# Whole-row value groups in the small attention: one group of values per key tile behind two rounds of scores and maxima

## The chip, the core and the metric

The kernel runs on one core of one Trainium2 chip. The metric is device time of one execution in microseconds (us), from the first to the last instruction of the core. The engines are TensorE (PE; its weight loads are PEld), VectorE (DVE), ScalarE (ACT), GpSimd (POOL) and SyncE (SP), which issues most DMAs. TensorE's clock is granted at 1.2 or 2.4 GHz; "granted clock 1.00" is 2.4.

## The reference, cut to what matters

Four sequences of S = 512 tokens, D = 256 features, pass through six blocks: a transformer block with rotary attention and 16 experts, a small attention, the first block again, a recurrent "thought" block, a windowed attention, and the thought block again. The change lies in the small attention:

```python
x = x + _L0_attn_ref(_layernorm(x, axis=-1), ...)
# in it: 32 query heads, 8 key/value heads, head size 8, no mask
q = q.reshape(B, S, 32, 8).transpose(0, 2, 1, 3)
k = jnp.repeat(k, 4, axis=1); v = jnp.repeat(v, 4, axis=1)
scores = jnp.einsum('bhqd,bhkd->bhqk', q, k) * scale
attn = jax.nn.softmax(scores, axis=-1)
out = jnp.einsum('bhqk,bhkd->bhqd', attn, v)
return out @ Wo + bo
```

## The kernel before

A plan (`Plan`) is written first: a list of steps in one order. Each engine's program then walks the same list and issues what it has to do for each step, so the order of the list is the order on every engine, and each engine waits in order. PSUM has eight banks of 128 partitions by 512 fp32 values.

The small attention (`small_attention`) works on batch b (4), query-head group qt (4), key/value head kv = 2 qt + g (8), key tile kt (T = 4 tiles of 128 keys), and r (KV = 4), the four query heads that share kv. Heads are eight wide (SD = 8), and the parts of the split fp32 operands are stacked to 24 rows, so that four matmuls for r = 0 to 3 fit into the four groups of 32 rows of TensorE's array and run side by side.

- `attend` (matmul at L1630): scores of one key tile (128 partitions) against all 512 queries, 26 rows, with the stored maxima among them, into a bank of `tring` (three banks, 3 to 5). ScalarE takes the exponential into a slot of `prT` (12 slots, L1844) and frees the bank.
- `maximum` (L1618): scores of a query tile against all keys, 24 rows, into a bank of `sring` (three banks, 0 to 2). VectorE reduces each to its maximum (L2034) and frees the bank. Maxima run ahead of the attends by a lead of 48. After 32 of them VectorE splits them into parts (L2040 to L2043), and four rounds' steps later TensorE turns them (`store_maxima`, L1624) through the single bank of `wring` (bank 7); ScalarE (L1840) and a DMA of POOL store them. In batch 0, four extra maxima follow each qt.
- `value` (L1641): the values, 32 columns wide for each r, so that four matmuls stand side by side in the four column groups, 128 rows deep, against the exponentials. They add up over four key tiles in the one bank of `oring` (bank 6), and in fp32 each is two records of the trace. In front of them, for kt > 0, stand matmuls of bf16 zeros (L1639), which add nothing to the sum. After the last key tile ScalarE copies the bank to `o_sb` (L1848).
- `finish` (L1649): four transposes of `o_sb` through `wring`, then VectorE divides by the row sums (L2049, L2051).
- Side work, one step of a generator `beside()` after every second attend: the products and values of the next batch (`small_product` L1599 to L1603, whose last, L1603, is followed by ScalarE's and VectorE's parts L1836 and L2022 out of `wring`; `small_values` L1609 to L1611; `feature` L1521), and the output products of the last batch (`small_out`, L1656 to L1658). All of it uses `wring`.

The inner loop yields after each attend; one maximum follows it, and after r = 1 and r = 3 a side step. Then `tick()` counts down the list `later` and runs what is due. The two halves of the values of key tile kt are due at the third and fourth tick after the last attend of kt. So the order on TensorE is: half 0, two scores and two maxima, side step, half 1, two scores and two maxima, side step. The halves are queries 0 to 255 and 256 to 511. Each half of kt > 0 has eight zero matmuls of 256 columns, two rounds over the four column groups.

Of the kernel before, what the change touches and what calls it, by code (L numbers as in the profile page):

```python
# [8 lines left out]
B, S, D = 4, 512, 256  # L9
T = S // P  # L10
# [4 lines left out]
KV = 4  # L15
# [13 lines left out]
VR = 32  # L29
# [123 lines left out]
def cols(c0, n):  # L153
    return slice(c0, c0 + n)


class Plan:
# [791 lines left out]
    def small_attention(self, ph, ahead):  # L949
# [5 lines left out]
        A = Phase()  # L955
# [14 lines left out]
        s = self.step("small_constants", A)  # L970
        s.after, s.count = self.boundary, self.count(f"p{ph}_const")
        const = s.count.up(64)
        s = self.step("small_fill", A)
# [15 lines left out]
        s = self.step("small_bias", A)  # L989
# [29 lines left out]
        s = self.step("small_ones", A)  # L1019
# [6 lines left out]
        stack_ready, stack_read, v_aug_of, v_ready, o_tm_of, o_made, nm_done = {}, {}, {}, {}, {}, {}, {}  # L1026
# [117 lines left out]
        later = []  # L1144
# [8 lines left out]
        def attend(b, qt):  # L1153
            if qt == 0:
                o_tm_of[b], o_made[b] = o_tm.take(), None
            otm, va = o_tm_of[b], v_aug_of[b]

            def value(kv, kt, exps, ob, half):
                if not ob:
                    ob.append(oring.take())  # L1160
                s = self.step("value", A)
                s.kv, s.kt, s.exps, s.use, s.va, s.v_ready, s.half = kv, kt, exps, ob[0], va.ap, [v_ready[b]], half
                s.o = None
                if half == 0:
                    return
                weighed = s.use.full if kt == T - 1 else self.values_weighed.up()
                for pt, _ in exps:
                    pt.users.append(weighed)
                if kt == T - 1:
                    s.o = o_sb.take()  # L1170
                    if kv % 2 and qt == 3:
                        stack_read[b] = s.use.full
                        va.users.append(s.use.full)
                    later.append([2, lambda: finish(kv, s.o, s.use.free)])

            def finish(kv, o, copied):
                s = self.step("finish", A)
                s.kv, s.o, s.copied, s.use, s.rr, s.otm = kv, o, copied, wring.take(), rsum.take(), otm
                o.users.append(s.use.full)
                s.inverted = self.vector_made.up()  # L1180
                s.rr.users.append(s.use.free)
                o_made[b] = s.use.free

            for g in range(2):
                kv = qt * 2 + g
                ob = []
                for kt in range(T):
                    exps = []
                    for r in range(KV):
                        s = self.step("attend", A)  # L1190
                        s.b, s.kv, s.kt, s.r, s.ready = b, kv, kt, r, [nm_done[b, qt], ones_there]
                        s.use, s.pt = tring.take(), prT.take()
                        exps.append((s.pt, s.use.free))
                        pace[0] = s.use.free
                        if r == KV - 1:
                            for half in range(2):
                                later.append([2 + half, lambda kv=kv, kt=kt, exps=exps, ob=ob, half=half: value(kv, kt, exps, ob, half)])
                        yield
                        if r % 2:
                            tick()  # L1200
# [306 lines left out]
def tensor_program(pe, plan):  # L1507
# [4 lines left out]
    for s in plan.order:  # L1512
        A = s.of
# [3 lines left out]
        elif s.kind == "feature":  # L1517
            w.wait_ge(s.use.before)
            for t in range(T):
                w.wait_ge(s.ready[t])  # L1520
                ins = pe.transpose(s.use.ap[:, t * P:(t + 1) * P], s.srcs[t], ident[:, :])  # L1521
            ins.then_inc(s.use.full[0].sem)

        elif s.kind in ("q_product", "q_rotate"):
# [5 lines left out]
            for k in range(KC):  # L1530
# [3 lines left out]
                ins = pe.matmul(use.ap[:, 0:n], hi, wlo[:, k, cols(c0, n)], start=False, stop=k == KC - 1)  # L1534
            ins.then_inc(use.full[0].sem)

        elif s.kind == "q_turn":
            w.wait_ge(s.use.before, s.ready)
            for j in range(QW // P):
                ins = pe.transpose(s.use.ap[:, j * P:(j + 1) * P], s.tm.ap[:, j * P:(j + 1) * P], ident[:, :])  # L1540
            ins.then_inc(s.use.full[0].sem)

        elif s.kind == "k_turn":
            w.wait_ge(s.use.before)
            for g in range(A.nk):
                ins = pe.transpose(s.use.ap[:, g * P:(g + 1) * P], s.tm.ap[:, QW + g * P:QW + (g + 1) * P], ident[:, :])
            ins.then_inc(s.use.full[0].sem)

        elif s.kind == "scores":
# [5 lines left out]
            for i, (qp, kp) in enumerate(((0, 0), (4, 0), (0, 1))):  # L1555
                for h in s.heads:
                    rows = slice(0, P) if A.wide else cols(h.j % 2 * A.hd, A.hd)
                    at = qp + (h.j if A.wide else (o.g * KV + h.j) // 2)
                    ins = pe.matmul(h.use.ap[:, 0:n], q[rows, at, :], k[rows, kp, o.g, keys], start=i == 0, stop=i == 2)  # L1559
# [3 lines left out]
        elif s.kind == "turn":  # L1563
            o = s.o
            w.wait_ge(s.use.before)
            for j in range(KV):
                w.wait_ge(o.norms[j])
                ins = pe.transpose(s.use.ap[:, j * P:(j + 1) * P], o.probs[j].ap[:, s.kt * P:(s.kt + 1) * P], ident[:, :])  # L1568
# [63 lines left out]

        elif s.kind == "value":
            w.wait_ge(s.use.before, A.zeroed, *s.v_ready)
            part = cols(s.half * S // 2, S // 2)
            for j, (pt, made) in enumerate(s.exps):
                if j == 0 and s.kt:
                    for i in range(2 * KV):
                        pe.matmul(s.use.ap[cols(i % KV * VR, VR), part], A.zero[:, 0:VR], A.zero[:, part], start=False, stop=False)  # L1639
                w.wait_ge(made)  # L1640
                ins = pe.matmul(s.use.ap[VR * j:VR * (j + 1), part], s.va[:, s.kt, s.kv, :], pt.ap[:, part],  # L1641
                                start=s.kt == 0 and s.half == 0, stop=s.kt == T - 1 and s.half == 1)
            if s.half:
                ins.then_inc(s.use.full[0].sem if s.kt == T - 1 else plan.values_weighed.sem)

        elif s.kind == "finish":
            w.wait_ge(s.use.before, s.copied)
# [995 lines left out]
```

## Time and profile before

| | us |
|---|---|
| median of 3 runs | 3684.36 (3679.31 to 3690.25) |
| the profiled execution, its span | 3687.3 |
| PE busy | 3303.7 (90%) |
| DVE busy | 2631.0 (71%) |
| ACT busy | 1933.5 (52%) |
| POOL busy | 990.3 (27%) |
| TensorE's mean granted clock | 0.938 |

The profiled execution was not timed apart from its span. Busy times are unions over the span; a matmul's time holds its latency, so a busy TensorE is not one at its peak. "Idle before" is an engine's idle time just ahead of an instruction, with the instruction of another engine that ended it; "issue" is a wait for nothing that the profile shows. In the timeline each line is a group of like instructions: start, time from the first start to the last end, engine, line of the kernel, operation, output and input, and the count.

### The profile page before, as it was taken

How to read it: one execution, taken by the hardware profiler on the slowest of the kernel's cores; microseconds unless marked ns; L12 is line 12 of the kernel's file. 1: busy time of each engine (PE TensorE's matmuls, PEld its weight loads, DVE VectorE, ACT ScalarE, POOL GpSimd, SP SyncE). 2: the span in 40 equal slices, each digit the busy share in tenths (PEclk: the TensorE clock that was granted, in tenths of full speed). 3: DMA queues.
4: the chain of work that ended last, by engine and by line, in shares of the span. 5: the costliest groups of instructions: out<-in, count | busy, mean ns of one | idle time of the engine just before them, and what ended most of it. 6: DMA issues, size and time to landing. Idle time of an engine off the chain costs nothing. (4 is left out here: it accounts for less than half of the span.)

```text
span 3687.3 us, 65201 instructions
## 1 busy us (share of the span) xinstructions
PE 3303.7 (90%) x22154; PEld 2194.8 (60%) x22154; DVE 2631.0 (71%) x8703; ACT 1933.5 (52%) x5275; POOL 990.3 (27%) x960
## 2 busy tenths in 40 slices
PE   6999999987997899997899999988799749999975
PEld 4666767664554344445667667665455437887853
DVE  5888888885444788873788888887344567777755
ACT  4667767664222366774676767666222125555531
POOL 3211112233454001012121212143444332222213
PEclk8999999998998689997999999998899769999986
DMA  4140500013755322302060500011756300000010
GB/s 129 52 170 7 166 1 1 20 48 110 178 91 116 70 46 58 73 23 72 1 220 1 172 1 1 4 48 57 215 88 122 89 1 15 1 16 4 1 34 23
DMA packets 202239, 234.78 MB, mean 64 GB/s; under 512 B 20662, under 2 KB 188536, under 8 KB 201080
## 3 DMA queue, kind: packets, MB, share of 16 engines
q1 hardware_dynamic: 170968, 190.48, 17.0%
q0 software_dynamic: 30944, 40.14, 6.5%
q8 instruction: 181, 2.97, 0.3%
q14 instruction: 146, 1.20, 0.1%
HBM read 98.13 MB, written 133.73 MB: 63 GB/s over the span
## 5 line engine op out<-in xcount | busy, mean ns | idle before, releaser
L1816 ACT ACTIVATE p_prob<-bank,p_small 128x256 f32<-128x256 f32 (+3 forms) x1280 | 646.2, 515 | 156.0 <-DVE p_small L1988 151.3
L1988 DVE CUSTOM_DVE_ANT_0 bank<-bank,p_mask 128x256 f32<-128x256 f32 (+3 forms) x1280 | 579.0, 490 | 97.1 <-PE bank L1559 85.7
L2336 POOL TENSOR_TENSOR p_tm<-p_rope_a,p_rope_b 128x512 f32<-128x512 f32 x192 | 245.8, 1280 | 1269.0 <-DVE p_rope_b L1968 1264.5
L1559 PE MATMUL bank<-p_k,p_q 64*128 64x256 f32 (+3 forms) x3840 | 529.2, 347 | 13.6 <-ACT p_prob L1816 12.5
L1821 ACT ACTIVATE p_prT<-bank 128x512 f32<-128x512 f32 x752 | 426.0, 601 | 211.5 <-PE bank L1568 209.6
L1568 PE MATMUL bank<-g_ident,p_prob 128*128 128x128 f32 x3008 | 438.3, 284 | 54.4 <-DVE p_prob L1997 20.8
L1997 DVE TENSOR_SCALAR p_prob<-p_prob,p_small 128x256 f32<-128x256 f32 (+3 forms) x1280 | 424.5, 395 | 11.3
L1577 PE MATMUL bank<-p_prT,p_v 128*64 128x512 f32 (+1 forms) x1504 | 428.2, 619 | 0.3 <-ACT p_prT L1821 0.3
L1568 PEld LDWEIGHTS bank<-g_ident,p_prob 128*128 128x128 f32 x3008 | 330.0, 142 | 150.6 <-issue 50.2
L1559 PEld LDWEIGHTS bank<-p_k,p_q 64*128 64x128 f32 (+1 forms) x3840 | 339.1, 188 | 116.1 <-issue 65.1
L2034 DVE TENSOR_REDUCE p_nmax<-bank 128x1 f32<-128x512 f32 x512 | 320.8, 683 | 56.8 <-PE bank L1618 54.6
L1844 ACT ACTIVATE p_prT<-bank 128x512 f32<-128x512 f32 x512 | 278.1, 597 | 132.1 <-PE bank L1630 129.7
L1751 PE MATMUL bank<-p_w,p_hT 128*128 (+1 forms) x632 | 325.7, 598 | 0.1
L1532 PE MATMUL bank<-p_w_hi,p_aT_hi 128*128 128x512 f32 (+1 forms) x768 | 287.5, 374 | 5.5 <-DVE p_aT_lo L1930 4.6
L1816 ACT ACTIVATION_READ_ACCUMULATOR p_prob<-bank,p_small 128x1 f32 x1280 | 267.3, 209 | 0.0
L1533 PE MATMUL bank<-p_w_hi,p_aT_lo 128*128 128x512 f32 (+1 forms) x768 | 266.4, 347 | 0.0
L1534 PE MATMUL bank<-p_w_lo,p_aT_hi 128*128 128x512 f32 (+1 forms) x768 | 265.9, 346 | 0.0
L1825 ACT ACTIVATE p_oT_hi<-bank 128x512 fp32r<-128x512 f32 x192 | 114.8, 598 | 242.1 <-PE bank L1577 240.3
L1589 PE MATMUL bank<-p_o_hi,p_oT_hi 128*128 128x256 f32 x768 | 226.4, 295 | 5.8 <-DVE p_oT_lo L2002 5.8
L1965 DVE TENSOR_TENSOR p_rope_a<-bank,p_cos 128x512 f32<-128x512 f32 (+1 forms) x384 | 186.7, 486 | 62.4 <-PE bank L1534 60.8
L1577 PEld LDWEIGHTS bank<-p_prT,p_v 128*64 128x64 f32 (+1 forms) x1504 | 126.7, 148 | 169.4 <-issue 161.1
L1590 PE MATMUL bank<-p_o_hi,p_oT_lo 128*128 128x256 f32 x768 | 216.7, 282 | 0.0
(288 smaller groups left out, 6215.8 us busy)
## 6 DMA issues: line engine op xcount, KB each, us to landing
sorted<-p_blank SPq DMA_DIRECT2D x32, 2304.0 KB, 19.2
p_w<-in_L_ffn_w SPq DMA_DIRECT2D x96, 256.0 KB, 4.5
p_h_in<-sorted SPq DMA_DIRECT2D x158, 144.0 KB, 2.7
p_k_st<-k_saved SPq DMA_DIRECT2D x16, 288.0 KB
p_q_st<-q_saved SPq DMA_DIRECT2D x16, 288.0 KB
g_stage<-in_L_ffn_wq SPq DMA_DIRECT2D x8, 512.0 KB, 3.8
g_stage<-in_L_ffn_wo SPq DMA_DIRECT2D x16, 256.0 KB, 4.3
q_saved<-p_qp SPq DMA_DIRECT2D x16, 256.0 KB, 3.2
```

Of the source, the lines that this page charges most:

```text
L1532: pe.matmul(use.ap[:, 0:n], hi, whi[:, k, cols(c0, n)], start=k == 0, stop=False)
L1533: pe.matmul(use.ap[:, 0:n], lo, whi[:, k, cols(c0, n)], start=False, stop=False)
L1559: ins = pe.matmul(h.use.ap[:, 0:n], q[rows, at, :], k[rows, kp, o.g, keys], start=i == 0, stop=i == 2)
L1568: ins = pe.transpose(s.use.ap[:, j * P:(j + 1) * P], o.probs[j].ap[:, s.kt * P:(s.kt + 1) * P], ident[:, :])
L1577: ins = pe.matmul(s.use.ap[cols(o.g * A.hd, A.hd), :], o.u.v.ap[:, o.k0 + kt, cols(o.g * A.hd, A.hd)], o.prT[kt].ap, start=kt == 0, stop=k ...
L1751: ins = pe.matmul(o.up.ap, o.hT.ap[:, k * P:(k + 1) * P], w_all(A)[:, bass.ds(at + k * 2 * H, 2 * H)], start=k == 0, stop=k == KC - 1)
L1816: act.activation(s.prob.ap[:, 0:s.o.w], s.use.ap[:, 0:s.o.w], ACT.Exp, bias=sm[:, 0, j:j + 1], scale=-1.0, accum_out=sm[:, 1, j:j + 1]).th ...
L1821: act.activation(s.prT.ap, s.use.ap, ACT.Copy).then_inc(s.use.free[0].sem)
L1844: act.activation(s.pt.ap, s.use.ap, ACT.Exp).then_inc(s.use.free[0].sem)
L1988: dve.tensor_tensor_reduce(x, x, A.mask[:, A.mask.shape[1] - o.w:], -1.0, FAR, ALU.add, ALU.min, o.sm.ap[:, 0, h.j:h.j + 1]).then_inc(made)
L1997: dve.tensor_scalar(o.probs[j].ap[:, 0:o.w], o.probs[j].ap[:, 0:o.w], o.sm.ap[:, 2, j:j + 1], None, ALU.mult).then_inc(made)
L2034: dve.tensor_reduce(A.nmax[:, s.qt % 2, s.t, s.r, s.g % 2:s.g % 2 + 1], s.use.ap, axis=AX.X, op=ALU.max, negate=True).then_inc(s.use.free[ ...
```

## The change

The two halves of `value` become one step, due at the third tick. It issues one round of four zero matmuls of 512 columns for kt > 0 (in place of four rounds of four with 256 columns), then four value matmuls over all 512 queries. Nothing else is touched: the rings, the number of rounds, the lead and the side steps stay. `finish` is still put into `later` by the step of the last key tile, which now runs one tick earlier.

```diff
-            def value(kv, kt, exps, ob, half):
+            def value(kv, kt, exps, ob):
                 if not ob:
                     ob.append(oring.take())
                 s = self.step("value", A)
-                s.kv, s.kt, s.exps, s.use, s.va, s.v_ready, s.half = kv, kt, exps, ob[0], va.ap, [v_ready[b]], half
+                s.kv, s.kt, s.exps, s.use, s.va, s.v_ready = kv, kt, exps, ob[0], va.ap, [v_ready[b]]
                 s.o = None
-                if half == 0:
-                    return
...
                         if r == KV - 1:
-                            for half in range(2):
-                                later.append([2 + half, lambda kv=kv, kt=kt, exps=exps, ob=ob, half=half: value(kv, kt, exps, ob, half)])
+                            later.append([2, lambda kv=kv, kt=kt, exps=exps, ob=ob: value(kv, kt, exps, ob)])
...
         elif s.kind == "value":
             w.wait_ge(s.use.before, A.zeroed, *s.v_ready)
-            part = cols(s.half * S // 2, S // 2)
+            if s.kt:
+                for i in range(KV):
+                    pe.matmul(s.use.ap[cols(i * VR, VR), :], A.zero[:, 0:VR], A.zero[:, :], start=False, stop=False)
             for j, (pt, made) in enumerate(s.exps):
-                if j == 0 and s.kt:
-                    for i in range(2 * KV):
-                        pe.matmul(s.use.ap[cols(i % KV * VR, VR), part], A.zero[:, 0:VR], A.zero[:, part], start=False, stop=False)
                 w.wait_ge(made)
-                ins = pe.matmul(s.use.ap[VR * j:VR * (j + 1), part], s.va[:, s.kt, s.kv, :], pt.ap[:, part],
-                                start=s.kt == 0 and s.half == 0, stop=s.kt == T - 1 and s.half == 1)
-            if s.half:
-                ins.then_inc(s.use.full[0].sem if s.kt == T - 1 else plan.values_weighed.sem)
+                ins = pe.matmul(s.use.ap[VR * j:VR * (j + 1), :], s.va[:, s.kt, s.kv, :], pt.ap,
+                                start=s.kt == 0, stop=s.kt == T - 1)
+            ins.then_inc(s.use.full[0].sem if s.kt == T - 1 else plan.values_weighed.sem)
```

## Rows read from the trace of the kernel before

**Rows 1.** Windows: length, busy us (instructions) by engine, PEclk, DMA share, GB/s.

```profile
1249.70:1694.70 445.00, 419.99 (x4984) 200.65 (x4983) 333.79 (x636) 306.91 (x577) 51.06 (x78) 0.94 0.20 47
1522.95:1533.84 10.89, 10.47 (x149) 4.96 (x148) 10.23 (x18) 8.69 (x17) 0.00 (x0) 1.00 0.77 191
```

**Rows 2.** Timeline of one clean pair; start, us, engine, line, operation, count.

```profile
1522.95 0.40 PE L1639 MATMUL bank<-p_zero 128*32 128x256 bf16 x8
1523.18 0.60 PE L1641 MATMUL bank<-p_prT,p_v_aug 128*32 128x256 f32 x8
1523.72 0.50 PE L1618 MATMUL bank<-p_k_st,p_q_st 24*128 24x512 f32 x1
1524.15 0.40 PE L1639 MATMUL bank<-p_zero 128*32 128x256 bf16 x8
1524.27 1.90 DVE L2034 TENSOR_REDUCE p_nmax<-bank 128x1 f32<-128x512 f32 x3 [0.28 <-PE bank L1618]
...
1525.45 0.40 PE L1639 MATMUL bank<-p_zero 128*32 128x256 bf16 x8
```

**Rows 3.** Groups by line, 1260 to 1690: count, busy us, mean ns, idle before.

```profile
L2034 DVE TENSOR_REDUCE p_nmax<-bank 128x1 f32<-128x512 f32 x448 | 281.6, 683 | 52.5 <-PE bank L1618 50.3
```

**Rows 4.** Timeline where extra maxima follow one another.

```profile
1306.43 6.87 DVE L2034 TENSOR_REDUCE p_nmax<-bank 128x1 f32<-128x512 f32 x11
...
1309.65 0.18 PEld L1618 LDWEIGHTS bank<-p_k_st,p_q_st 24*128 24x128 f32 x1 [0.50 <-DVE p_nmax L2034]
```

**Rows 5.** Waits (us, times, longest), then TensorE's timeline with side work.

```profile
PEld bank L1641 <- ACT p_o_sb L1848: 14.2, 22, 0.8
...
1547.16 0.30 PE L1609 MATMUL bank<-p_w_hi,p_uT_hi 128*128 128x64 f32 x1
...
1547.95 0.40 PE L1639 MATMUL bank<-p_zero 128*32 128x256 bf16 x8
...
1567.07 0.50 PE L1630 MATMUL bank<-p_q_st,p_k_st 26*128 26x512 f32 x1
...
1568.03 0.49 PE L1618 MATMUL bank<-p_k_st,p_q_st 24*128 24x512 f32 x1
...
1569.73 0.39 PE L1656 MATMUL bank<-p_w_hi,p_oT_hi 128*128 128x256 f32 x1
...
1570.63 0.64 PE L1641 MATMUL bank<-p_prT,p_v_aug 128*32 128x256 f32 x8
```

**Rows 6.** Timeline of a bias product with `finish` behind it.

```profile
1503.47 0.39 PE L1603 MATMUL bank<-p_ones,p_b_st 2*64 2x512 f32 x1
...
1504.64 0.59 ACT L1836 ACTIVATE p_qp<-bank 64x512 fp32r<-64x512 f32 x1
...
1505.26 0.68 DVE L2022 SCALAR_TENSOR_TENSOR p_qp<-bank,p_qp 64x512 fp32r<-64x512 f32 x1 [0.27 <-ACT p_qp L1836]
...
1505.99 0.66 PE L1649 MATMUL bank<-g_ident,p_o_sb 128*128 128x128 f32 x4 [1.05 <-DVE p_qp L2022]
```

**Rows 7.** Windows around changes of the granted clock.

```profile
1200.00:1250.00 50.00, 37.28 (x99) 18.51 (x101) 44.64 (x106) 7.20 (x11) 5.66 (x7) 0.53 0.45 101
...
1307.60:1311.30 3.70, 3.29 (x29) 1.36 (x32) 3.70 (x7) 2.05 (x4) 0.00 (x0) 1.00 0.80 171
...
1312.50:1316.80 4.30, 4.00 (x46) 1.49 (x43) 2.91 (x6) 2.84 (x6) 0.00 (x0) 0.60 0.10 23
...
1341.50:1352.00 10.50, 10.47 (x133) 4.84 (x132) 9.49 (x20) 7.60 (x15) 2.22 (x4) 1.00 0.02 5
...
1366.66:1381.70 15.04, 13.62 (x97) 5.57 (x96) 10.10 (x21) 7.41 (x14) 2.22 (x4) 0.51 0.02 3
...
1645.00:1656.80 11.80, 11.32 (x151) 5.16 (x150) 3.08 (x15) 9.76 (x20) 5.33 (x8) 1.00 0.02 4
```

**Rows 8.** Timeline at half clock.

```profile
1251.49 1.08 PE L1641 MATMUL bank<-p_prT,p_v_aug 128*32 128x256 f32 x8
...
1252.51 0.79 PE L1618 MATMUL bank<-p_k_st,p_q_st 24*128 24x512 f32 x1
```

## Prediction

> **What bounds the kernel now.** I read the windows first, then the groups by line, then the timeline of the one stage that the change touches, tile by tile. The values are computed only in the small attention, between 1249.7 and 1694.7 us of the 3687.3 us span: 445 us, with TensorE busy 420, VectorE 334, ScalarE 307, mean granted clock 0.94 [rows 1]. Whatever the change does must come out of these 445 us; the other 3242 us keep their instructions and their order.
>
> TensorE looks like the bound (94% busy), but its busy time counts latency. A stretch without side work shows what sets the pace: the eight half-groups of kv 1522.95 to 1533.84 take 10.89 us, with VectorE busy 10.23 us of them [rows 1]. There is one `value` half per round of scores and maxima, and the pair of halves of one key tile takes 1522.95 to 1525.45, 2.50 us [rows 2]. Four reduces at 0.63 us of engine time each (281.6 us / 448) are 2.51 us [rows 3]. So in clean stretches the maxima on VectorE set the pace already; TensorE alone would need 2 x 1.20 = 2.40 us (zeros 0.23, values 0.54, scores 0.43 from start to start [rows 2]). Only where side work (products, transposes, output products) stands between the rounds is TensorE itself the bound.
>
> **The change part by part.** Call A the round with r = 0, 1 and B that with r = 2, 3, each two scores and two maxima. Before: values half 0, A, side slot 1, values half 1, B, side slot 2. After: whole values, A, side slot 1, B, side slot 2. There are 128 key tiles, hence 128 such pairs (1024 fp32 value matmuls of 256 queries, two records each; 1536 zero matmuls).
>
> *Zeros.* 96 key tiles have them. Before, a half has 8 matmuls x 256 columns, four column groups side by side, and costs 0.23 us: 0.46 us a tile. After, 4 x 512 columns in one round: the same columns per group as one half, so 0.23 us. TensorE is spared 0.23 us a tile. Off TensorE nothing changes.
>
> *Values.* A half costs 0.54 us to the next scores, of which 4 x 256 columns at 2.4 GHz (two records deep, two passes each) are 0.43 and 0.11 is the turn to the scores. A whole is 0.85 + 0.11 = 0.96, behind zeros 1.19 us. Bounds: 1.07 us (no turn, no start-up) and 1.37 us (two halves as now), 0.12 us below and 0.18 us above; I take 1.19 because half-clock rows (1.08 us for eight records against 0.60) scale with the columns and not with the instructions [rows 2, 8].
>
> *Scores.* One turn scores-to-values (0.43 - 0.21 = 0.22 us) and one back (0.11) disappear per tile. With the zeros that is 0.56 us a tile for TensorE alone, 2.40 to about 1.85 us. If TensorE were the only bound this would be some 65 us.
>
> *Where the gain goes.* The maxima have three PSUM banks (`sring`), the scores three (`tring`). Two adjoining rounds need four of each. The second maximum of B takes the bank of the first maximum of A, and TensorE is in order, so it waits for that reduce. From the rows: scores start 1523.72, reduce starts 1524.27, 0.55 us later [rows 2]; one reduce lasts 0.68; the weight load follows 0.06 us behind the freed bank. The last is seen where extra maxima stand in a row: the eleven reduces from 1306.43 are 0.62 us apart, the fifth ends at 1309.59, and the next load starts at 1309.65, waiting for VectorE [rows 4]. So B's last maximum starts 0.55 + 0.68 + 0.06 = 1.29, say 1.30 us behind A. Behind it the values queue (0.43 later), and behind the values (1.19) the next A. A clean pair becomes 1.30 + 0.43 + 1.19 = 2.92 us, whatever TensorE saved. VectorE has its four reduces from 0.55 to 3.11 us (0.68 + 3 x 0.62) and the next fill at 2.92 + 0.55 = 3.47: it now idles 0.36 us per pair. The bound has become a loop from bank to bank. On ScalarE the same loop is 0.53 + 0.60 + 0.06 = 1.19 us, just under it; it governs the last pairs, where the maxima have ended. The Trainium skill, TensorEngine Tiling, "PSUM Bottleneck" and the first of its gotchas, says that tiled matmuls move the bottleneck to the copies out of PSUM and that row tiling presses on the banks. By that rule alone nothing is gained in clean stretches; by the same page's "Key Properties", that a change of tiling mode drains the engine, the turns saved would count. The trace agrees with both (0.22 and 0.11 us of turn, and the waits for L2034).
>
> *Pair by pair*, from the timeline (S-to-S starts; d1, d2 are the side work in the slots). After = values + max(1.30, 0.43 + d1) + 0.43 + d2.
> - 17 clean pairs at 2.50: 2.92, +7.1. Five more behind the last maxima, 2.43 to 2.81: +1.9.
> - 7 pairs with VectorE's three small maxima parts, 2.88 to 3.0: +0.8.
> - 13 pairs with the last key tile, 2.99: the second 0.5 us there is the next values' wait for the single output bank (14.2 us over 22 waits [rows 5]). It goes, since two rounds now hide the 0.6 us copy, but the pair is 2.92 (2.81): -1.1.
> - 17 pairs with the first key tile (no zeros, 1.00 us) and the `finish` transposes, 2.89. One tick earlier, `finish` now falls into slot 1, inside the bank wait, and is free: 1.00 + 1.30 + 0.43 = 2.73: -2.7.
> - 9 pairs with products in both slots (0.79 to 0.84 each [rows 5]), about 4.06 to 3.73: slot 1 lies inside the wait, slot 2 in full: -3.0.
> - 9 pairs with output products in slot 2 alone (0.90 [rows 5]), 3.41 to 3.82, 4.33 to 4.78: +3.5.
> - 10 pairs with the store of maxima (L1624 splits A by 0.96 [rows 5]), 7 up 0.15, 3 with products down 0.35: 0.
> - 6 pairs where the bias product (L1603) is followed by `finish`, 4.02 us. `finish` needs the one `wring` bank, which ScalarE and VectorE must empty first: L1603 at 1503.47, ScalarE's part at 1504.64, VectorE's ends 1505.94, transposes 1505.99, a wait of 1.05 us behind B [rows 6]. Now `finish` is asked for in slot 1, ahead of B, and holds B up: 1.61 (A's two exponentials) + 0.55 + 0.68 puts it 2.85 us behind A, then 0.59 + 0.43 + 1.06, with 1.00 of values: 4.9 us. +5.4. Behind `finish` are queued B's four matmuls, and VectorE starves with them.
> - The rest (transposes in slot 1, -1.2; output products with `finish`, -0.9; three pairs with four extra maxima of batch 0, +1.5; bias product alone, +0.6; eight half-clock pairs, +2.4): +2.4.
>
> Sum: +14.3 us at the clock of before.
>
> *The clock.* It falls to 1.2 GHz behind stretches with little TensorE work: 1307.60 to 1311.30 (3.7 us with one half of values) is followed by 0.60 in 1312.50 to 1316.80, and 1362.99 to 1366.66, a stretch like it, by 0.51 over 15 us [rows 7]. There are four such stretches in the timeline, where batch 0 has its extra maxima; three were followed by a fall, one (1337.86) was not: 1.00 in 1341.50 to 1352.00 [rows 7]. A fall costs 1.3 to 5.6 us (the half-clock pairs against like pairs), 3.2 on the mean. The six `finish` pairs now have 3.9 us without values each; I count three more falls, +10 us.
>
> The profiled execution spans 3687.3 us, within the runs' 3679.3 to 3690.3 and 0.08% over their median, so I add to the median: 3684.4 + 14.3 + 10 = 3709 us, some 0.7% slower.
>
> **The rivals.**
> 1. *The gain arrives* (faster). If the second maximum of B did not wait (rounds spread by side work, or reduces that run ahead), clean pairs stay at VectorE's 2.50, last-tile and first-tile pairs fall to 2.50 (30 x 0.45 = 14 us), and the 35 pairs with side work fall by 0.5 (17 us): -31 us, 3653 us. For it: VectorE is only 75% busy in the stage. Against: three banks and four maxima are in the code, and the wait is in rows 4. It decides if B's last maximum starts under 0.9 us behind A, where the clean pair is 2.50.
> 2. *It cancels* (no change). The value group at its low bound (-0.12 x 128 = -15 us) and no more falls: 3684 us.
> 3. *The clock gives way.* Values and zeros are the matmuls over all 128 rows; they stream 0.85 + 0.43 of a clean pair's 2.50 us now (0.51), 0.85 + 0.21 of 2.92 then (0.36), since half the zeros are gone and the pair is longer; with scores alone the clock stood at 0.53 over 1200 to 1250 while TensorE was 75% busy [rows 7]. At half clock zeros and values are 0.43 + 1.71 + 0.15 = 2.29, the bank loop 0.86 (0.55 and the scores' 0.79 us against 0.50 [rows 2, 8]) + 0.68 + 0.06 = 1.60, scores 0.73: 4.62 us a pair, +1.70. With 40% of the pairs there: +87 us, about 3785 us. Against: the clock held 1.00 in 1645.00 to 1656.80, with two matmuls a round [rows 7]. The Trainium skill, TensorE: Matmul & The Clock Gate, "A second HAM failure mode: psum-queue depth-cycling", says that small idles between groups that cycle through PSUM banks make the clock swing; this change makes just such idles. By that rule the time would be this rival's.
> 4. *It doesn't do what it says*: then L1639 would not show x384 and L1641 not x1024. The diff leaves no room for that, and it gets no chance.
>
> **How the numbers follow.** Forecast (+12 to +45 us) 0.50; rival 1 0.16; rival 2 0.20; rival 3 0.14. The predicted time is the first's, 3709. The values' upper bound (0.18 x 128 = 23 us) and eight falls in all (25 us) make 3746; on top the range goes on into rival 3, to 3768. Below, it takes in rival 2 and a third of rival 1's gain, 3674. A difference of 0.3% (11 us) is about what a measurement of this kernel can tell from no change. Faster 0.17, same 0.20, slower 0.63.
>
> **What would show it.** L1639 x384 at 512 columns, L1641 x1024. Right: the last L1618 of B starting 1.3 us behind A with its load waiting for L2034; clean pairs of 2.9 us; VectorE idle about 0.36 us a pair before L2034; L1848 no longer ahead of L1641; L1649 waiting some 2 us for L2022 six times. Wrong: clean pairs of 2.5 us, or a mean clock in the stage under 0.85.

## The result and the profile after

The changed kernel takes 3733.99 us (median of 4 runs, 3728.65 to 3737.49), the kernel before 3686.8 us on the same chip (4 runs): a ratio of 1.0132, 95% interval 1.0114 to 1.0151, slower by 47 us. The forecast was 3709 us, slower by 25 us (by 22 us once the kernel before has its fourth run). The direction and the range held; the size was half of what came. The slowdown is 1.3%, clear of no change by its interval but small.

The page of the changed kernel (busy us and share of the span; then by line: busy us, mean ns, idle before):

```profile
span 3726.9 us, 60853 instructions
PE 3316.3 (89%) x19976; PEld 2160.4 (58%) x19978; DVE 2628.5 (71%) x8703; ACT 1931.7 (52%) x5275; POOL 991.6 (27%) x960
...
L2029 DVE TENSOR_REDUCE p_nmax<-bank 128x1 f32<-128x512 f32 x512 | 320.5, 683 | 86.7 <-PE bank L1615 85.8
```

TensorE has 2178 instructions fewer and is busy 12.6 us longer. VectorE's reduces (L2034 before, L2029 now) cost the same, but VectorE idles 86.7 us ahead of them; before it was 56.8.

The stage, from the first to the last value matmul, and parts of it (length, busy us by engine, granted clock):

```profile
1256.20:1743.50 487.30, 432.42 (x2808) 166.85 (x2807) 332.85 (x636) 302.44 (x577) 51.13 (x78) 0.87 0.19 43
1256.20:1360.00 103.80, 91.68 (x570) 34.75 (x569) 76.72 (x143) 59.24 (x112) 6.68 (x12) 0.86 0.23 51
1360.00:1450.00 90.00, 79.87 (x447) 27.87 (x445) 60.95 (x110) 48.62 (x93) 6.68 (x12) 0.72 0.18 40
1450.00:1545.00 95.00, 85.24 (x640) 36.75 (x639) 79.64 (x154) 65.74 (x127) 9.83 (x17) 1.00 0.12 26
1545.00:1700.00 155.00, 137.26 (x983) 56.51 (x981) 113.90 (x225) 104.05 (x204) 22.14 (x36) 0.96 0.22 52
1700.00:1743.50 43.50, 38.37 (x184) 10.97 (x176) 1.65 (x6) 24.79 (x45) 5.81 (x2) 0.57 0.11 31
```

It is 487.3 us long where it was 445.0 [rows 1], 42 us more; the profiled span grew by 39.6 us (the stage starts 6 us later, and the rest behind it is 9 us shorter; neither holds changed code). The clock is 0.87 in place of 0.94. Since the clock has two levels, (1 - clock) x 2 x length is the time at 1.2 GHz: 127 us of the stage now, 53 us before (the clock's two digits leave some 5 us open; its own records in the traces add up to 130 and 49 us).

**A clean pair at full clock.** In the timeline of the changed kernel (start, us, what it is, count, idle before) L1634 are the zeros, L1637 the values, L1627 the scores, L1615 the maxima:

```profile
1505.78 0.40 PE L1634 MATMUL bank<-p_zero 128*32 128x512 bf16 x4
1506.01 1.03 PE L1637 MATMUL bank<-p_prT,p_v_aug 128*32 128x512 f32 x8
...
1508.71 0.40 PE L1634 MATMUL bank<-p_zero 128*32 128x512 bf16 x4
1508.94 1.03 PE L1637 MATMUL bank<-p_prT,p_v_aug 128*32 128x512 f32 x8
...
1509.90 0.49 PE L1615 MATMUL bank<-p_k_st,p_q_st 24*128 24x512 f32 x1
...
1510.49 2.06 ACT L1839 ACTIVATE p_prT<-bank 128x512 f32<-128x512 f32 x4 [0.86 <-PE bank L1627]
1511.14 0.50 PE L1627 MATMUL bank<-p_q_st,p_k_st 26*128 26x512 f32 x1 [0.52 <-ACT p_prT L1839]
1511.21 0.50 PE L1615 MATMUL bank<-p_k_st,p_q_st 24*128 24x512 f32 x1
1511.64 0.40 PE L1634 MATMUL bank<-p_zero 128*32 128x512 bf16 x4
```

The pair is 2.93 us (1505.78 to 1508.71 and again to 1511.64); the forecast was 2.92. Zeros cost 0.23, values 0.96. The wait in the second of the two pairs: round A starts at 1509.90; the last maximum of round B starts 1.31 us later, and the zeros and values behind it 0.43 us after that. Ahead of it stands a score that waits for ScalarE: the exponential's bank comes free at 1.24 us, the maximum's at 1.3.

**Half clock.** A like pair, 139 us earlier:

```profile
1366.53 0.62 PE L1634 MATMUL bank<-p_zero 128*32 128x512 bf16 x4
1366.92 1.93 PE L1637 MATMUL bank<-p_prT,p_v_aug 128*32 128x512 f32 x8
1368.78 0.79 PE L1627 MATMUL bank<-p_q_st,p_k_st 26*128 26x512 f32 x1
...
1370.32 0.79 PE L1627 MATMUL bank<-p_q_st,p_k_st 26*128 26x512 f32 x1 [0.32 <-ACT p_prT L1839]
1370.39 0.79 PE L1615 MATMUL bank<-p_k_st,p_q_st 24*128 24x512 f32 x1
1371.10 0.62 PE L1634 MATMUL bank<-p_zero 128*32 128x512 bf16 x4
```

It is 4.57 us (forecast 4.62), 1.64 us more. Of 127 pairs 28 are at half clock; in the kernel before it was 11 (counting only pairs that are at half clock for more than half of their length, 26 and 10).

**The `finish` behind the bias product** (L1644 the transposes, L2017 VectorE's part of the product):

```profile
1531.31 0.39 PE L1600 MATMUL bank<-p_ones,p_b_st 2*64 2x512 f32 x1
...
1532.47 0.58 ACT L1831 ACTIVATE p_qp<-bank 64x512 fp32r<-64x512 f32 x1
1533.09 0.68 DVE L2017 SCALAR_TENSOR_TENSOR p_qp<-bank,p_qp 64x512 fp32r<-64x512 f32 x1 [0.26 <-ACT p_qp L1831]
...
1533.83 0.66 PE L1644 MATMUL bank<-g_ident,p_o_sb 128*128 128x128 f32 x4 [2.13 <-DVE p_qp L2017]
```

TensorE stands for 2.13 us where it stood for 1.05 [rows 6]; the pair, 1529.97 to 1534.85, is 4.88 us (forecast 4.9). Another of the six, with the same wait, is 5.65 us long because the clock falls in the middle of it, at 1434.0:

```profile
1434.71 1.12 PE L1644 MATMUL bank<-g_ident,p_o_sb 128*128 128x128 f32 x4 [2.15 <-DVE p_qp L2017]
```

The four transposes take 1.12 us there and not 0.66.

### The profile page after: what moved, and what is told of

It reads as the page before. It is cut to its first block and busy times, and to the rows that moved or that the text cites. A ratio compares the mean times of both kernels' runs of the same rounds, so it can differ in the third digit from the quotient of the medians.

```text
span 3726.9 us, 60853 instructions
## 1 busy us (share of the span) xinstructions
PE 3316.3 (89%) x19976; PEld 2160.4 (58%) x19978; DVE 2628.5 (71%) x8703; ACT 1931.7 (52%) x5275; POOL 991.6 (27%) x960
## 5 line engine op out<-in xcount | busy, mean ns | idle before, releaser
L2029 DVE TENSOR_REDUCE p_nmax<-bank 128x1 f32<-128x512 f32 x512 | 320.5, 683 | 86.7 <-PE bank L1615 85.8
```

The lines of the kernel that those rows point to most:

```text
L2029: dve.tensor_reduce(A.nmax[:, s.qt % 2, s.t, s.r, s.g % 2:s.g % 2 + 1], s.use.ap, axis=AX.X, op=ALU.max, negate=True).then_inc(s.use.free[ ...
```

## The experiments

The ratio of each run is to the kernel before on the same chip. Three chips were used: the first for e1 to e4, the second for e5 to e8, the third for e9 to e11. On the last two the kernel before itself took 3723 us and not 3684 (the same instructions), so of whole times only ratios are compared. The stage can be compared across chips: the changed kernel's is 487.3 us in the first profile and 483.5 on the third chip (e11), while the rest of the execution is 3240 and 3270 us. A time that was expected is set against 3684 us times the ratio. "At half clock" is worked out from the stage's window as above. Two theories of the clock stood against each other, beside the bank loop that both share: that the clock follows the zero columns (theory 1), or the idle time behind the bank wait (theory 2).

**e1, e7, e10: the kernel before with other numbers of zeros.**

```diff
-                    for i in range(2 * KV):
+                    for i in range(KV):       # e1; e7: range(3 * KV); e10: the whole "if j == 0 and s.kt" left out
```

> The kernel before (values in two halves), with one round of four zero matmuls of 256 columns ahead of each half in place of two. Both theories: clean pairs stay at 2.50 us, since VectorE's four reduces set them; a pair with products in both slots goes from 4.1 to 3.9 us. Theory 1, the bank loop costs at full clock and the missing zeros cost the clock: half-clock pairs, 12 in the kernel before, rise towards the 28 of the changed kernel, and the time is 3700 to 3720 us. Theory 2, the idle time behind the bank wait and not the zeros costs the clock: half-clock pairs stay near 12, and the time is 3675 to 3685 us, the saved zeros where side work binds (about 40 pairs by 0.2 us).

> The kernel before with three rounds of zeros of 256 columns ahead of each half in place of two (e1 had one). Theory 1, that the clock follows the zero columns: e1 21, before 11, so about 5 half-clock pairs here, 8 us less, against 0.21 us more for each of 96 pairs that TensorE bounds (up to 20 us): 3685 to 3697 us. Theory 2: half-clock pairs unchanged from 11, 3697 to 3705 us.

> The kernel before without any zeros. Theory 1: the clock follows the zero columns (three rounds 11 half-clock pairs, two 11, one 21), so 35 or more half-clock pairs here and 1.003 to 1.010 of the kernel before, though TensorE is spared 0.46 us in each of 96 pairs. Theory 2: half-clock pairs near 11 to 15, and a ratio under 0.997, since side pairs fall by 0.46 us and clean pairs to VectorE's 2.39.

Ratios: none 1.0096 (1.0061 to 1.0131), one round 1.0018 (1.0001 to 1.0035), three 1.0026 (1.0010 to 1.0041). The stage of e10, no zeros (window: length, busy us by engine, granted clock):

```profile
1276.70:1740.60 463.90, 441.18 (x3448) 184.40 (x3447) 332.85 (x636) 306.01 (x577) 51.08 (x78) 0.81 0.20 45
```

The stage of e1, one round:

```profile
1257.40:1708.40 451.00, 426.09 (x4216) 193.93 (x4215) 333.07 (x636) 306.68 (x577) 51.08 (x78) 0.89 0.20 46
```

The stage of e7, three rounds:

```profile
1266.20:1727.70 461.50, 436.99 (x5752) 218.77 (x5751) 337.75 (x636) 306.83 (x578) 51.17 (x78) 0.94 0.20 46
```

At half clock: 176, 99, 53 (before, two rounds) and 55 us with 0, 1, 2 and 3 rounds. The profiled execution of e10 is the fastest of its four (granted clock 0.919 over the whole execution; the others 0.909 to 0.919), so 176 is rather low. The zeros add nothing to the result and cost TensorE time, and without them the kernel is 1% slower: theory 1, which had expected 1.003 to 1.010 where theory 2 expected less than 0.997. A third round buys nothing more: e7's ratio lies in theory 1's range, but its time at half clock did not fall as theory 1 said. The size in e1 came out smaller than theory 1 said: 3693 us lies between the ranges of both theories and is hardly clear of no change, since TensorE's 0.11 us a half is saved meanwhile and clean pairs fell from 2.50 to 2.39 us, where 2.50 was expected.

**e2: the change with two rounds of zeros ahead of the values**, so with as many zero columns as before.

```diff
-                for i in range(KV):
-                    pe.matmul(s.use.ap[cols(i * VR, VR), :], ...
+                for i in range(2 * KV):
+                    pe.matmul(s.use.ap[cols(i % KV * VR, VR), :], ...
```

> The changed kernel with two rounds of four zero matmuls of 512 columns instead of one, so as many zero columns as before, directly ahead of the values. Both theories: clean pairs 3.14 us (2.93 + 0.21), and so 96 x 0.21 = 20 us more at an equal clock. Theory 1 (missing zeros cost the clock): half-clock pairs fall from 28 to about 12, 25 us less, the time 3725 to 3733 us. Theory 2 (the waits cost it): half-clock pairs stay near 28 and the time is 3745 to 3758 us.

Ratio 1.0107 (1.0082 to 1.0131), 3723.05 us.

```profile
1256.60:1746.30 489.70, 432.18 (x3192) 172.29 (x3191) 333.63 (x636) 301.62 (x577) 51.15 (x78) 0.92 0.18 42
```

Clean pairs are 3.14 us as expected, the time at half clock falls from 127 to 78 us, half-clock pairs from 28 to 16. Each of 96 pairs is 0.21 us dearer, 20 us in all, and yet the stage is only 2 us longer: what the zeros cost they give back. Theory 2 expected 3745 us or more and is out by over 10 us.

**e3: the one round of zeros moved into the bank wait**, between A and B of the tile before.

```diff
+                            if kt:
+                                later.append([1, lambda ob=ob: zeros(ob)])
                             later.append([2, lambda kv=kv, kt=kt, exps=exps, ob=ob: value(kv, kt, exps, ob)])
...
-            if s.kt:
-                for i in range(KV):
-                    pe.matmul(s.use.ap[cols(i * VR, VR), :], A.zero[:, 0:VR], A.zero[:, :], start=False, stop=False)
...
+        elif s.kind == "zeros":
+            for i in range(1 * KV):
+                pe.matmul(s.use.ap[cols(i % KV * VR, VR), :], A.zero[:, 0:VR], A.zero[:, :], start=False, stop=False)
```

> The changed kernel, with its one round of zeros moved between the two rounds of scores of the tile before, where TensorE waits for the bank of the first maximum. The bank loop says: the zeros are hidden there and a clean pair goes from 2.93 to 2.70 us; pairs with products in both slots stay at 3.7 us. That is 80 pairs x 0.23 = 18 us less at an equal clock: 3716 us. If the second round's wait were not what I say (a free bank, another releaser), the pair would stay at 2.93 or grow by the added turn of the array, 3734 to 3750 us. The clock: theory 1 expects no change in the half-clock pairs (the zeros are the same), theory 2 fewer of them (the idle gap is broken up), which would make it 3700 us.

Ratio 1.0147 (1.0115 to 1.0179), 3733.14 us. In its timeline (L1639 values, L1645 zeros, L1632 scores, L1620 maxima):

```profile
1556.92 1.06 PE L1639 MATMUL bank<-p_prT,p_v_aug 128*32 128x512 f32 x8
1557.91 0.49 PE L1632 MATMUL bank<-p_q_st,p_k_st 26*128 26x512 f32 x1
...
1558.35 0.40 PE L1645 MATMUL bank<-p_zero 128*32 128x512 bf16 x4
...
1559.15 0.50 PE L1632 MATMUL bank<-p_q_st,p_k_st 26*128 26x512 f32 x1
1559.22 0.49 PE L1620 MATMUL bank<-p_k_st,p_q_st 24*128 24x512 f32 x1
...
1559.64 1.07 PE L1639 MATMUL bank<-p_prT,p_v_aug 128*32 128x512 f32 x8
```

The pair is 2.72 us, and B's last maximum stands 1.31 us behind A with the zeros in between: in a clean pair the zeros were free, and the loop is where the forecast put it. Yet the time is no better than the changed kernel's. The stage is 492.8 us at a clock of 0.83, 168 us at half clock: zeros stand in the idle gap, and the time at half clock did not shrink but grew. The granted clock of its four executions, 0.919 to 0.925 against the changed kernel's 0.925 to 0.928, says the same. Theory 2, which expected 3700 us, is out by this too, and theory 1's expectation of an unchanged clock was not met either. Why the same zeros kept the clock less well here is open.

**e4: whole values one tick later.**

```diff
-                            later.append([2, lambda kv=kv, kt=kt, exps=exps, ob=ob: value(kv, kt, exps, ob)])
+                            later.append([3, lambda kv=kv, kt=kt, exps=exps, ob=ob: value(kv, kt, exps, ob)])
```

> The changed kernel with the whole values due one tick later, between rounds A and B of the tile after next, where half 1 stood; the rounds that adjoin are then B and the next A. By the bank loop the clean pair is the same 2.93 us (the wait has moved into the next A). Output products, which stand in slot 2, now lie in the wait: nine pairs of 3.82 fall to 2.95, -8 us. The finish behind the bias product is back behind B, so its wait for the bank of the products is 1 us and no longer 2: six pairs from 4.9 to 5.6 fall to about 4, -6 us. At an equal clock 3720 us; with fewer falls behind those six pairs 3700 to 3710 us. The rival, that the adjoining rounds cost nothing and all of the loss is in where the values stand, expects 2.5 us pairs and 3680 us.

Ratio 1.0064 (1.0044 to 1.0084), 3707.01 us: by the ratios 25 us faster than the changed kernel. Clean pairs are 2.93 us, pairs with output products 2.97 in place of 3.82, as expected. The stage:

```profile
1258.60:1729.00 470.40, 427.71 (x2804) 165.69 (x2803) 330.36 (x633) 303.04 (x575) 51.15 (x78) 0.86 0.19 44
```

It is 17 us shorter at much the same clock (132 us at half). That much hung on which slot of side work lies in the wait and where `finish` stands: 14 us were expected of the output products and of `finish`, and pairs with the store of maxima, which I had left out, fell too, from 3.86 to between 2.93 and 3.30 us mostly. The time lies in the range of 3700 to 3710 us, but not for the reason given: `finish` waits at most 0.7 us for the products' bank where it waited 2.1, and the time at half clock stayed. Fewer falls were expected and did not come. The other 8 of the 25 us show only in the ratios: the profiled executions differ by 19 us.

**e5, e6: one tick later, with two and three rounds of zeros in the wait.** e3's step `zeros` with `range(2 * KV)` and `range(3 * KV)`, due at 2, the values at 3.

> Whole values one tick later (as in e4) and two rounds of four zero matmuls of 512 columns, moved into the bank wait between round B and the next A; as many zero columns as in the kernel before, where e4 has half. Both theories: two rounds of zeros fit into the wait (0.43 + 0.43 + the turns of 0.33 against 1.31 us), so the clean pair is 2.74 us, e4's 2.93 less the 0.2 of its zeros. At an equal clock 3692 us. Theory 1 (the missing zero columns cost the clock): half-clock pairs fall from e4's 31 to about 16, 3667 to 3672 us, faster than the kernel before. Theory 2 (the waits, not the zeros): they stay near 30, 3690 us.

> As e5 with three rounds of zeros in the wait. The third round no longer fits wholly where side work stands in the same slot: clean pairs 2.74 to 2.84 us, pairs with side work in slot 2 0.2 us longer than e5's. Theory 1: half-clock pairs under 10, 3665 to 3675 us. Theory 2: still near 30, 3700 us.

Ratios 0.9997 (0.9973 to 1.0021) and 1.0019 (0.9996 to 1.0043). The window of e5's stage:

```profile
1276.70:1718.70 442.00, 416.46 (x3188) 153.21 (x3187) 332.96 (x633) 305.31 (x575) 51.11 (x78) 0.95 0.20 47
```

One of e5's clean pairs in the timeline, 2.74 us:

```profile
1654.77 1.07 PE L1639 MATMUL bank<-p_prT,p_v_aug 128*32 128x512 f32 x8
...
1656.20 0.62 PE L1645 MATMUL bank<-p_zero 128*32 128x512 bf16 x8
...
1657.51 1.06 PE L1639 MATMUL bank<-p_prT,p_v_aug 128*32 128x512 f32 x8
```

The window of e6's stage:

```profile
1272.30:1729.40 457.10, 433.41 (x3572) 159.84 (x3571) 334.50 (x633) 306.57 (x575) 51.19 (x78) 0.95 0.20 46
```

With as many zero columns as before, 44 us are at half clock (46 with three rounds) in place of e4's 132, and the whole values are level with the kernel before. Against e4 the ratio falls by 0.0067, 25 us, and the stage by 28 us. The clock alone accounts for that: 88 us less at half clock are some 32 us, at the 36% that a half-clock pair loses (next section). So hiding the zeros gave nothing in sum: clean pairs have 0.19 us less than e4's, but first key tiles with `finish` went from 2.73 to 2.99 us and six of the nine pairs with output products from 2.97 to 3.32, since there the wait was in use already. Theory 1 expected a kernel faster than before (ratios of 0.995 to 0.998 for both); it came out level, and that part was wrong.

**e8: VectorE's reduces over half of the columns.** The maxima are then taken over the first 256 keys only; that half of the work is left out.

```diff
-s.use.ap, axis=AX.X, op=ALU.max,
+s.use.ap[:, 0:S // 2], axis=AX.X, op=ALU.max,
```

> The changed kernel with VectorE's reduces over the first 256 of 512 columns only; so the maxima are over half of the queries' keys, which changes what is computed and leaves half of that work out. A reduce goes from 0.68 to about 0.42 us and the maxima's bank loop from 1.29 to 1.03 us. The scores' loop over ScalarE is 0.53 + 0.60 + 0.07 = 1.20 and then sets the start of B's second half: clean pairs 1.21 + 0.07 + 0.43 + 1.19 = 2.9 us, unchanged or 0.05 less, though VectorE has lost over a third of its work in the stage. The rival, that VectorE's total work in the stage is what bounds, expects clean pairs of 2.4 us or less.

One execution was timed, at 3736.82 us (the kernel before: 3723.15 on this chip). The reduce is 0.42 us, VectorE's busy time in the stage 219 us in place of 333, and clean pairs are 2.85 us (1497.24 to 1500.09):

```profile
1497.24 0.40 PE L1634 MATMUL bank<-p_zero 128*32 128x512 bf16 x4
...
1498.43 0.50 PE L1615 MATMUL bank<-p_k_st,p_q_st 24*128 24x512 f32 x1
1499.67 0.49 PE L1627 MATMUL bank<-p_q_st,p_k_st 26*128 26x512 f32 x1 [0.51 <-ACT p_prT L1839]
...
1500.09 0.40 PE L1634 MATMUL bank<-p_zero 128*32 128x512 bf16 x4
```

A third less work on VectorE gives 0.08 us of 2.93. VectorE's load isn't the bound of a clean pair; the round trip of three banks is, and with short reduces it is the scores' over ScalarE. Elsewhere the reduces do count: the stage is 465.1 us, some 20 us shorter than the changed kernel's at much the same clock, and pairs with four extra maxima in a row fall from 5.28 to 3.97 us.

```profile
1262.50:1727.60 465.10, 413.27 (x2808) 157.84 (x2807) 218.65 (x635) 300.99 (x578) 51.23 (x78) 0.88 0.19 45
```

**e9: e5 without its zeros where a side step precedes them.**

```diff
             def zeros(ob):
-                self.step("zeros", A).use = ob[0]
+                if self.order[-1].kind in ("maximum", "attend", "value"):
+                    self.step("zeros", A).use = ob[0]
```

> As e5 (whole values one tick later, two rounds of zeros in the bank wait), but the zeros are left out where a side step has just filled that slot: there they stood behind the side work and on the path (3.32 us in e5 where 2.75 would do). Some 20 pairs by 0.57 us, -11 us against e5 at an equal clock, a ratio to the kernel before of 0.997. Theory 1 holds that the side matmuls, over all 128 rows themselves, keep the clock in place of the zeros: half-clock pairs stay near e5's 11. If the clock needs the zeros there too, half-clock pairs rise above 16 and the ratio is 1.000 to 1.003.

Ratio 1.0044 (1.0019 to 1.0069).

```profile
1279.00:1740.00 461.00, 431.87 (x2772) 162.70 (x2771) 330.23 (x633) 306.65 (x575) 50.98 (x78) 0.85 0.19 45
```

The stage has 416 TensorE instructions fewer than e5's (2772 against 3188), so 52 tiles of 96 lost their zeros and not 20. Some 20 of them have side work in the slot, as meant; 31 have `finish`, which the condition leaves out as well. The pairs became shorter as expected (output products 3.32 to 2.77 us, first key tiles with `finish` 2.99 to 2.73), but 138 us are at half clock, and the ratio lies above both ranges expected. So the side matmuls and the transposes, though they run in the same slots, did not stand in for the zeros: that part of theory 1 was wrong. As one more count of zero columns the run falls in line, under half of e5's zeros and three times its half-clock time.

**e11: the changed kernel again, on the chip of e9 and e10.**

> The changed kernel itself once more, on this chip, to have its half-clock pairs a second time (28 of 127 in the first profile). Theory 1: 24 to 35 of them, stage 480 to 495 us, ratio 1.010 to 1.015. If the first profile was an accident of the clock, the count is near 12 and the ratio near 1.006.

Ratio 1.0121 (1.0094 to 1.0149).

```profile
1271.10:1754.60 483.50, 428.10 (x2808) 167.25 (x2807) 332.90 (x636) 301.98 (x577) 51.01 (x78) 0.88 0.19 43
```

116 us at half clock, 26 half-clock pairs: the first profile was no accident.

The last column but one is the granted clock over whole executions, as a mean over all runs of the kernel, less that of the kernel before on the same chip (for the first profile's kernel, less the one profile of before).

| | zero columns per group and tile | stage us | at half clock us | clock, difference | ratio |
|---|---|---|---|---|---|
| e10, halves | 0 | 463.9 | 176 | -0.022 | 1.0096 |
| e1, halves | 512 | 451.0 | 99 | -0.007 | 1.0018 |
| before, halves | 1024 | 445.0 | 53 | 0 | 1 |
| e7, halves | 1536 | 461.5 | 55 | +0.003 | 1.0026 |
| after, whole | 512 | 487.3 | 127 | -0.011 | 1.0132 |
| e11, whole, again | 512 | 483.5 | 116 | -0.010 | 1.0121 |
| e3, whole, in the wait | 512 | 492.8 | 168 | -0.015 | 1.0147 |
| e4, whole, later | 512 | 470.4 | 132 | -0.010 | 1.0064 |
| e9, whole, later, in the wait | 1024 in 44 of 96 tiles | 461.0 | 138 | -0.011 | 1.0044 |
| e2, whole | 1024 | 489.7 | 78 | -0.001 | 1.0107 |
| e5, whole, later, in the wait | 1024 | 442.0 | 44 | -0.001 | 0.9997 |
| e6, whole, later, in the wait | 1536 | 457.1 | 46 | +0.001 | 1.0019 |

## Why the prediction was right in its direction and half in its size

*What comes out of the stage.* Right: the stage grew by 42 us and the profiled span by 39.6.

*The value group at 0.96, the zeros at 0.23, the wait of 1.30 us, the pair of 2.92.* Right: 0.96, 0.23, 1.31, 2.93. In none of the changed kernel's 110 pairs with four maxima does the last maximum start less than 1.31 us behind the first matmul of its two rounds. e3 and e4 found the wait again at 1.31; with e8's short reduces the least is 1.18, so it is a round trip and not a load. Which engine frees the last bank was told less well: at B the score's wait for ScalarE (1.24) and the maximum's for VectorE (1.3) are 0.07 apart.

*Pair by pair.* Right. Forecast and measured at full clock: clean 2.92, 2.93; first key tile with `finish` 2.73, 2.73; products in both slots 3.73, 3.71 to 3.85; output products in slot 2 3.82, 3.83; behind the last maxima 2.81, 2.85; `finish` behind the bias product 4.9, 4.88 in the two of the six that are at full clock. The other four, 5.16 to 6.13 us, hold a piece at half clock, and what they have too much is the clock's. The prediction's working of the 4.9 has a 1.06 too many: as written it makes 5.9. Its four real terms, 1.00 + 2.85 + 0.59 + 0.43, make 4.87, and the trace has 0.99, 2.87, 0.58 and 0.44. The sum of +14.3 us holds as well: of the stage's 42 us the clock takes 27 (next point), and 15 are left. The signs held too: the values no longer wait for the copy to `o_sb`, and `finish` waits six times for the products' bank, 12.8 us on TensorE in all. VectorE idles 30 us more ahead of its reduces, where 0.36 us in each of 110 pairs would be 40.

*The clock.* This is the step that failed: the term was put at three more falls of 3.2 us, +10 us, and it measured 27. In the trace 74 us more of the stage are at half clock (127 against 53), and since a pair there takes 4.57 for 2.93 us, 36% of that time is lost: 27 us. (Each half-clock pair set against a like pair at full clock gives the same: some 48 us lost now, 21 before.) The number of falls was nearly right: the granted clock falls nine times in the stage now and five times before. Five of the nine begin in pairs where `finish` stands behind another user of `wring` (at 1300.9, 1416.9, 1434.0, 1550.1 and 1635.4), much as I had said, but these last 31 us together. What failed is the length: the five falls of the kernel before lasted 3.4 to 17.1 us, 41 in all, and the nine now 3.4 to 37.5 us, 123 in all. The longest of the kernel before, and the two longest now:

```profile
1367.10:1384.20 17.10, 15.69 (x116) 6.32 (x112) 10.48 (x22) 7.46 (x14) 2.22 (x4) 0.50 0.01 3
...
1352.10:1379.40 27.30, 26.02 (x120) 7.91 (x112) 15.26 (x29) 13.38 (x25) 2.23 (x4) 0.50 0.01 2
1700.30:1737.80 37.50, 33.06 (x138) 9.51 (x134) 1.10 (x4) 20.97 (x39) 5.81 (x2) 0.50 0.13 35
```

I had taken the size of a fall from a kernel with twice the zeros, where the clock comes back sooner [rows 7]. And the long waits for a bank do not carry the loss: the time at half clock is as long in e4, where the six waits are cut, and the longest fall stands where no bias product is near. What the clock hangs on was in rival 3, in the right words (half the zeros gone, scores alone leave the clock low), and got 0.14. The runs with other numbers of zeros show it: 0, 1, 2 rounds leave 176, 99, 53 us at half clock, and two rounds instead of one take the whole values from 127 to 78 us (e2) and, moved into the wait as well, from 132 to 44 us (e4, e5). The mean clock of all their executions agrees with the single profiles (table). The small idles that rival 3 also names do not carry it: e3 puts zeros into them and is at half clock for longer. Rival 3's price for a pair was right (4.62, measured 4.57), its extent not: 22% of the pairs, not 40%.

*VectorE as the pace of the clean pair before.* Wrong in its reason. I had four reduces at 0.63 us make 2.51. In e1 reduces stand back to back and ten take 6.07 us:

```profile
1643.29 6.07 DVE L2034 TENSOR_REDUCE p_nmax<-bank 128x1 f32<-128x512 f32 x10
...
1643.85 0.29 PE L1639 MATMUL bank<-p_zero 128*32 128x256 bf16 x4
...
1646.24 0.29 PE L1639 MATMUL bank<-p_zero 128*32 128x256 bf16 x4
```

That is (6.07 - 0.68) / 9 = 0.60 each, and e1's clean pair is 2.39 us, VectorE's true pace. The 2.50 before was TensorE's 1.20 in one half and a bank wait of 0.1 in the other. It changed no term, since 2.50 was measured.

*The rivals.* The gain of rival 1 never came: in no kernel with whole values and full reduces did the last of four maxima start under 1.3 us behind the first round (1.18 with e8's short reduces). Rival 2's low bound of the values was not met (0.96). Rival 4 is out: the trace has 1024 value records and 384 zeros.

No version beat the kernel before; e5 is level with it. 3734 lies in the range even without its part for rival 3 (up to 3746): eight falls, 25 us, had been allowed for there, close to the 27 that came, and 23 us for slower values that did not come.

## What to carry to other kernels

When work is gathered into larger groups to save turns of the array, count first how many outputs the next stretch needs at once and how many banks there are: with four wanted of three, the saving is paid back as one round trip through the engine that drains them, and the trace of before has every leg of it. Matmuls that add nothing may be paying for the clock; before taking them out, take the time at half clock from the windows, and price a fall from a kernel that has as little array work as the new one will have, not from the one that is fed. Work can be put into a wait for nothing as long as the wait is empty: in clean pairs the zeros, `finish` and the side products all were; where side work already filled it, the two rounds of e5 cost up to their full 0.55 us.

## What the hardware showed that I had not expected

- Zero matmuls of bf16, 32 columns wide and 128 rows deep, hold TensorE's clock: without them the stage of the kernel before is at half clock for 176 us and with two rounds a half for 53, and the kernel is 1% faster with them. More than 1024 columns a tile bought nothing. Only their number was varied; whether width, depth or type matters was not.
- The same zeros placed between two rounds of scores (e3) left more time at half clock (168 us) than directly ahead of the values (127, 116 us). The mean granted clock of its executions is lower as well (0.923 against 0.927). It is not explained.
- Reduces of 512 columns run 0.60 us apart when all their inputs are there, 0.62 to 0.63 in the groups of the kernel before; the duration of one, 0.68 us, is not its pace.
- The same kernel before took 3684 us on one chip and 3723 us on two others. For the changed kernel the difference lies outside the stage.
